# Index rows, broadcasts and network steps of a neighbour-attention kernel in another order, and the last activations on ScalarE and GpSimd

## What is computed

```python
# L0: for each point the 8 nearest points, then 4 blocks
idx = top_k(-d2(ctx), 8)
for i in range(4):
    p = where(points >= 0, points, 0.01 * points)          # the activation
    c = w_center[i] @ p                                     # here both weights are fside
    gn = w_neighbor[i] @ gather(p, idx)
    points = (c + gn.sum(over neighbours)) / 9 + points
# L1: for each point the 30 nearest points, a small network, attention
rel = pts[idx30] - pts                                      # 3 coordinates
feat = spherical(rel) and its difference from its mean      # sqrt, arctan
h = lrelu(bn(feat @ W1.T)); h = lrelu(bn(h @ W2.T)); h = lrelu(bn(h @ W3.T))
att = softmax(h); out = points + sum(att * points[idx30])
```

## Time and profile before

| what | value |
|---|---|
| median of 3 runs | 841.17 us (841.12 to 841.86) |
| the profiled execution | 846.98 us, its span 845.1 us |
| TensorE (PE) busy | 749.7 us, 89% |
| VectorE (DVE) busy | 656.1 us, 78% |
| ScalarE (ACT) busy | 260.7 us, 31% |
| GpSimd (POOL) busy | 175.3 us, 21% |
| mean granted TensorE clock | 0.949 of full speed |

### The profile page before, as it was taken

One profiled execution on the slowest core, in us unless ns is written; L12 is line 12 of the kernel. 1 busy time (PEld: TensorE's weight loads), 2 busy tenths in 40 slices (PEclk: granted clock), 3 DMA queues, 4 the chain that ended last, 5 costly groups with the idle time before them and its releaser, 6 DMA issues.

```text
span 845.1 us, 13319 instructions
## 1 busy us (share of the span) xinstructions
PE 749.7 (89%) x5530; PEld 611.5 (72%) x5530; DVE 656.1 (78%) x1057; ACT 260.7 (31%) x367; POOL 175.3 (21%) x134
## 2 busy tenths in 40 slices
PE   5979899698999999789899959794988999898988
PEld 3768788677778888678688747573876887676766
DVE  4757987969899999798897899677667878786701
ACT  7325642421551212100011221121232545454500
POOL 3113855861403113002200220121040000000000
PEclk9889899899999999999899998796999999999999
DMA  9520002020002000444430000000000455848581
GB/s 358 143 99 2 1 1 100 1 100 0 1 1 100 0 1 1 186 168 145 136 125 2 0 1 0 1 1 0 0 1 2 161 201 175 285 145 291 185 300 56
DMA packets 32700, 73.43 MB, mean 87 GB/s; under 512 B 11392, under 2 KB 11392, under 8 KB 30336
## 3 DMA queue, kind: packets, MB, share of 16 engines
q1 hardware_dynamic: 32496, 70.49, 23.9%
q10 hardware_dynamic: 144, 2.10, 0.6%
HBM read 49.37 MB, written 23.20 MB: 86 GB/s over the span
## 4 chain that ended last, share of the span: by engine, by line
PE 38%; DVE 37%; DMA 9%; ACT 7%; issue 6%; POOL 2%; SPq 0%; ACTq 0%; DVEq 0%; POOLq 0%
PE bank L1389 11%; DMA att_d<-scratch 6%; DVE scratch L937 5%; DVE idx L813 4%; DVE vals L811 4%; DVE scratch L881 3%; DVE pts_l L886 3%; PE bank L1417 3%; PE bank L1287 2%; PE bank L1368 2%; PE bank L1288 2%; PE bank L1289 2%; PE bank L1477 2%; PE bank L1369 2%; PE bank L1370 2%
## 5 line engine op out<-in xcount | busy, mean ns | idle before, releaser
L1389 PE MATMUL bank<-nbr,pts_l 128*128 128x512 f32 x1024 | 246.5, 399 | 10.5 <-DVE pts_l L886 8.2
L1389 PEld LDWEIGHTS bank<-nbr,pts_l 128*128 128x128 f32 x1024 | 194.5, 192 | 53.7 <-DVE pts_l L886 10.4
L461 POOL TENSOR_TENSOR pts_h<-scratch,pts_h 128x512 fp32r<-128x512 f32 x58 | 81.6, 1410 | 354.6 <-ACT pts_h L635 354.6
L1368 PE MATMUL bank<-wT,pts_h 128*128 128x512 f32 x256 | 105.7, 413 | 9.9 <-DVE pts_l L886 9.9
L635 ACT CAST pts_h<-scratch 128x512 fp32r<-128x512 f32 x58 | 35.9, 620 | 236.9 <-DVE scratch L881 236.9
L1369 PE MATMUL bank<-wT,pts_h 128*128 128x512 f32 x256 | 102.7, 401 | 0.0
L1370 PE MATMUL bank<-wT,pts_h 128*128 128x512 f32 x256 | 102.6, 401 | 0.0
L720 ACT COPY scratch<-bank 128x512 f32<-128x512 f32 x64 | 69.9, 1135 | 68.7 <-DMA att_d<-scratch 45.2
L1287 PE MATMUL bank<-pts_h 128*128 128x512 f32 (+2 forms) x192 | 74.5, 388 | 15.4 <-DVE pts_l L784 11.7
L642 ACT CAST pts_l<-bank 128x512 fp32r<-128x512 f32 x64 | 37.2, 588 | 135.9 <-PE bank L1370 135.7
L1288 PE MATMUL bank<-pts_l,pts_h 128*128 128x512 f32 (+2 forms) x192 | 71.0, 370 | 0.0
(11 more groups left out here) (189 smaller groups left out, 1214.4 us busy)
## 6 DMA issues: line engine op xcount, KB each, us to landing
att_d<-scratch SPq DMA_DIRECT2D x64, 256.0 KB, 2.5
nbr<-att_d SPq DMA_DIRECT2D x16, 1024.0 KB, 7.1
more<-a_rows SPq DMA_DIRECT2D x17, 480.0 KB, 4.5
scratch<-a_rows SPq DMA_DIRECT2D x15, 480.0 KB, 4.2
X<-in_ctx SPq DMA_DIRECT2D x12, 512.0 KB, 7.7
out_dram<-X SPq DMA_DIRECT2D x16, 256.0 KB, 4.6
more<-in_ctx SPq DMA_DIRECT2D x4, 512.0 KB, 7.8
scratch<-in_fside_BxSxS SPq DMA_DIRECT2D x2, 1024.0 KB, 13.5
```

The lines of the kernel that those rows point to most:

```text
L461: pool.tensor_tensor(p_l[:, t, hf * HALF:(hf + 1) * HALF], p32(n), p_h[:, t, hf * HALF:(hf + 1) * HALF].bitcast(F32), ALU.subtract).then_i ...
L1368: pe.matmul(bank[g % 3][:], p_h[:, t, cols], wT[:, 0, t, :], start=(t == 0), stop=False)
L1389: mm = pe.matmul(bank[3 + g % 3][:], y[:, m, t * P:(t + 1) * P], nbr[b][:, m, hf * HALF:(hf + 1) * HALF], start=(m == 0 and part_ == 0), s ...
```

## The change

Five things are changed.

1. The order of some calls in the set-up: `adj_turn(0)` behind `gram(2)`; on ScalarE `adjacency(1)` ahead of `mirror_out(2)`, `nbr_out(2)` behind the `high_half` copies, `adjacency(5)` and `mirror_out(9)` ahead of `gram_out(10)`, `gram_out(13)`, `mirror_out(13)` and `gram_out(14)` ahead of the first four `p_high`; on VectorE the first steps of `select` of tiles 6 and 7 behind the first four `p_make`.
2. `index_rows` at g = 36, 39, 42 and 52 with its turn one step later. SP stores the first three rows at once and starts the broadcasts then; only the broadcasts from u = 3 on wait for the whole selection. Each `lookup` waits for all four rows (`s_ar` at `CHUNKS`), `row_turned` is gone.
3. `NET` has 42 steps where it had 38: some pairs are split, an empty step stands ahead of each of the three sums, and a sum and its first reader share a step. With it `T0` goes from 109 to 113, `S0` from 115 to 119 and `S_END` from 26 to 18. The code of `FREE_AT`, `LOAD_AT` and `tail_groups` is not changed. Chunk 0 is then loaded behind q = 5, 9, 13 and 17 as before; chunk 1 behind 21, 25, 29 and 33 (before 27, 29, 31, 33), chunk 2 behind 37, 41, 45 and 49 (44, 46, 48, 50), chunk 3 behind 53, 57, 61 and 63 (59, 61, 63, 63).
4. For n >= 40 (the p of passes 5, 6 and 7) `p_make` is gone. ScalarE makes relu(x) and relu(-x/100), GpSimd subtracts them (`p_join`), and `p_high` and `p_low` follow one step later.
5. Waits that go with it (`s_sel` in `index_rows`, `s_wm` in `p_high`, `s_pr`).

```diff
+        N1 = 2 * CT * 5
+        def q32(n):
+            return more[:, 3, (n % 2) * HALF:(n % 2 + 1) * HALF]
-        R0 = 47
+        ROWS_AT = {36: 0, 39: 1, 42: 2, 52: 3}
+        TURN_AT = {g + 1: c for g, c in ROWS_AT.items()}
-        NET = [(0,), (1,), (2,), (3, 4), ((5, 0),), ((5, 1), (5, 2)), (6,), (7,), (8, (9, 0)), ((9, 1),),
-               ((9, 2), 10), (11,), (12, 13), (14, 15), (16,), (17, 18), (19,), (20, 21), (22,), (24,), (25,), (26,),
-               (27, 28), (29,), (30, 31), (32,), (33, 34), (35,), (37,), (38,), (39,), (40,), (41, 42), (44,), (45,),
-               (46,), (47,), (48,)]
+        NET = [(0,), (1,), (2,), (3, 4), ((5, 0),), ((5, 1),), ((5, 2),), (6,), (7,), (8,), ((9, 0),), ((9, 1),),
+               ((9, 2), 10), (11,), (12, 13), (14,), (15,), (16,), (17,), (18,), (19,), (20,), (21,), (22,), (),
+               (24, 25), (26,), (27, 28), (29, 30), (31, 32), (33, 34), (35,), (), (37, 38), (39,), (40,), (41, 42),
+               (), (44, 45), (46,), (47,), (48,)]
...
-            sp.wait_ge(s_adjT, TILES)
-            sp.wait_ge(s_sel, TILES)
             for c in range(CHUNKS):
-                sp.wait_ge(s_ar, c + 1)
-                sp.dma_start(a_rows[c], a_row[:]).then_inc(s_arow, 16)
-                sp.wait_ge(s_arow, 16 * (c + 1))
+                if c < CHUNKS - 1:
+                    sp.wait_ge(s_ar, c + 1)
+                    sp.dma_start(a_rows[c], a_row[:]).then_inc(s_arow, 16)
+            for c in range(CHUNKS):
                 for t in range(2 * CH):
                     u = 2 * CH * c + t
+                    if u == 0:
+                        sp.wait_ge(s_arow, 16 * (CHUNKS - 1))
                     if u == 3:
                         sp.wait_ge(s_sel, TILES)
+                    if u == 9:
+                        sp.wait_ge(s_ar, CHUNKS)
+                        sp.dma_start(a_rows[CHUNKS - 1], a_row[:]).then_inc(s_arow, 16)
+                    if u == 2 * CH * (CHUNKS - 1):
+                        sp.wait_ge(s_arow, 16 * CHUNKS)
...
+            def p_join(n):
+                pool.wait_ge(s_pr, 2 * (n - N1 + 1))
+                pool.tensor_tensor(p32(n), p32(n), q32(n), ALU.subtract).then_inc(s_p32, 1)
...
             mirror_out(1)
             gram_out(2)
             nbr_out(0)
+            adjacency(1)
             mirror_out(2)
-            adjacency(1)
...
-            nbr_out(2)
             for k in range(KT):
                 high_half(k, 1)
             mirror_out(6)
             gram_out(7)
+            nbr_out(2)
             adjacency(3)
...
             gram_out(9)
+            mirror_out(9)
             adjacency(4)
-            mirror_out(9)
+            adjacency(5)
+            gram_out(10)
+            mirror_out(10)
             nbr_out(4)
-            gram_out(10)
-            adjacency(5)
-            mirror_out(10)
...
+            def p_halves(n):
+                it = n // (2 * CT)
+                b, hf, t = it % B, (n % (2 * CT)) // CT, n % CT
+                if n == N1:
+                    act.wait_ge(s_look, 2 * TILES)
+                act.wait_ge(s_xu, 2 * CT * (it - 1))
+                act.wait_ge(s_p1, n - 1)
+                src = X[:, b, t, hf * HALF:(hf + 1) * HALF]
+                act.activation(p32(n), src, ACT.Relu).then_inc(s_pr, 1)
+                act.activation(q32(n), src, ACT.Relu, scale=-SLOPE0).then_inc(s_pr, 1)
...
             act.wait_ge(s_g, NT + 3)
+            gram_out(13)
+            mirror_out(13)
+            gram_out(14)
             for j in range(CT):
                 p_high(j)
-            gram_out(13)
+            mirror_out(14)
             adjacency(6)
-            mirror_out(13)
-            gram_out(14)
             adjacency(7)
-            mirror_out(14)
...
             select([4, 5])
-            select([6, 7], 0, 2)
...
             for n in range(CT):
                 p_make(n)
-            select([6, 7], 2, 3)
+            select([6, 7], 0, 3)
...
-                    if it + 1 < ITS:
+                    if it + 1 < ITS and 2 * CT * (it + 1) + j < N1:
                         p_make(2 * CT * (it + 1) + j)
...
             for n in range(CT):
                 w_turn(n)
+            gram(2)
             adj_turn(0)
-            gram(2)
...
-                pe.wait_ge(s_ar, row_turned(G0 + 1 + u // 2))
+                pe.wait_ge(s_ar, CHUNKS)
```

More of the change, by code:

```diff
@@ L201, in build @@
         s_p32 = sem("p_ready")
+        s_pr = sem("p_halves_ready")
         s_p0 = sem("p_high_ready")
@@ L287, in w_bank @@
             return bank[(6, 7, 4, 5, 0, 2, 6, 7)[n]][:]
-        def row_turned(g):
-            return min(max((g - R0 - 2) // 4 + 1, 0), CHUNKS)
         @block.sync
@@ L486, in _ @@
                     if s_ >= NT and it + 1 < ITS:
-                        p_low(2 * CT * (it + 1) + s_ - NT)
+                        n = 2 * CT * (it + 1) + s_ - NT
+                        if n < N1:
+                            p_low(n)
+                        else:
+                            p_join(n)
+                            if n % (2 * CT):
+                                p_low(n - 1)
+                            if n % (2 * CT) == 2 * CT - 1:
+                                p_low(n)
         @block.scalar
@@ L619, in _ @@
             gram_out(9)
+            mirror_out(9)
             adjacency(4)
-            mirror_out(9)
+            adjacency(5)
+            gram_out(10)
+            mirror_out(10)
             nbr_out(4)
-            gram_out(10)
-            adjacency(5)
-            mirror_out(10)
             gram_out(11)
             mirror_out(11)
-            norm_out(1)
             nbr_out(5)
             gram_out(12)
+            norm_out(1)
             mirror_out(12)
+            def p_halves(n):
[8 more added lines that the diff above has]
+                act.activation(q32(n), src, ACT.Relu, scale=-SLOPE0).then_inc(s_pr, 1)
             def p_high(n):
@@ L634, in p_high @@
                 act.wait_ge(s_p32, n + 1)
+                if n >= N1 and n % (2 * CT) == 0:
+                    act.wait_ge(s_wm, NT * (n // (2 * CT)))
                 act.copy(p_h[:, t, hf * HALF:(hf + 1) * HALF], p32(n)).then_inc(s_p0, 1)
@@ L665, in side @@
                     nbr_out(T)
-                if (g - R0) % 4 == 2 and 0 <= (g - R0) // 4 < CHUNKS:
-                    a_row_out((g - R0) // 4)
+                if g in TURN_AT:
+                    a_row_out(TURN_AT[g])
                 if g == 16 + NT:
@@ L751, in _ @@
                     if it + 1 < ITS:
-                        p_high(2 * CT * (it + 1) + j)
+                        n = 2 * CT * (it + 1) + j
+                        if n < N1:
+                            p_high(n)
+                        else:
+                            p_halves(n)
+                            if j:
+                                p_high(n - 1)
+                            if j == 2 * CT - 1:
+                                p_high(n)
                     side(16 * it + NT + j)
@@ L899, in index_rows @@
                 src = idx[:, CH * c:CH * (c + 1), :].rearrange("p t k -> p (t k)")
+                dve.wait_ge(s_sel, CH * (c + 1))
                 if c:
@@ L1158, in side @@
                     select_step(T, n)
-                if (g - R0) % 4 == 0 and 0 <= (g - R0) // 4 < CHUNKS:
-                    index_rows((g - R0) // 4)
+                if g in ROWS_AT:
+                    index_rows(ROWS_AT[g])
                 for u in (2 * (g - G0), 2 * (g - G0) + 1):
@@ L1399, in turn_a @@
                     pe.wait_ge(s_nbr, TILES)
-                u = min(2 * (R0 + 4 * c - G0), 2 * TILES - 2)
-                if u >= 0:
-                    pe.wait_ge(s_pick, u + 1)
                 pe.transpose(bank[6][:, 384:HALF], a_f, ident[:]).then_inc(s_aT, 1)
@@ L1433, in side @@
                     adj_turn(T)
-                if (g - R0) % 4 == 2 and 0 <= (g - R0) // 4 < CHUNKS:
-                    turn_a((g - R0) // 4)
+                if g in TURN_AT:
+                    turn_a(TURN_AT[g])
                 for u in (2 * (g - G0) - 2, 2 * (g - G0) - 1):
```

## The result

The changed kernel takes 838.68 us in the median (836.36 to 841.82, 20 runs), the kernel before, run on the same chip, 841.64 (837.48 to 846.3, 20 runs). The ratio is 0.996, with a 95% interval of 0.9944 to 0.9977: faster by some 3 us, where 10 were forecast. 838.68 lies inside the range, but nearer to no change than to the forecast. The profiled execution took 837.86 us, its span is 835.8.

A forecast was written before the change was run, and what follows sets the result against it. It saw six stretches with different limits: TensorE and VectorE full in selection, neither in lookups, TensorE partly waiting for VectorE in the network, TensorE limiting the last steps. -7 -11 -28 +36 = -10 gave 831 us, range 816 to 847.

The forecast's parts named there:

- the signs in the profile that it named: First `y_low` near 168, g 112 earlier, GpSimd some 35 us busier, four tail load waits of 6 to 8 us.
- set-up: Set-up to first `y_low`: reordered calls shorten TensorE's gaps, -3.5 -6.6 +3.5, about -7 us (bounds -3 to -10).
- rows and broadcasts: Lookups: earlier rows and broadcasts remove waits for the first broadcasts and `a_row_out`, about -11 us (-7 to -12).
- network and activation: Network and last 16 steps: 42 steps cut TensorE's idle time, -28 us, including net -2 for the moved activation.
- tail: Tail: four full TensorE stops at loads, 7.0 us each plus 2.4 of low clock; about +36 us (+23 to +45).
- The "-5" for waits that go: Tail: today's last wait (2.5 us) and some store waits vanish, since loads come every fourth spread; -5 us.
- The conversion to the runs' median: Whole kernel: the runs' median was taken as 5.8 us below the profiled 846.98, so 841.2 - 10 = 831.
- The rival of GpSimd's lock: Aggregate steps, passes 4 to 6: GpSimd's lock makes VectorE the bound; +6, 847 us; chance 0.18.
- part 3: Network and last 16 steps: `NET` with 42 steps shrinks TensorE's waits for VectorE; -28 us (bounds -5 to -45).
- Loads hidden anyway: Tail: ScalarE and SP run ahead of TensorE, so the four loads cost only 4; 799 us; chance 0.05.
- Gains cancel: Whole kernel: the passes' gain and the tail's loss cancel within 1.7 us; 841 us; chance 0.08.

The follow-up runs named there:

- the cut kernels: The kernel before and the changed kernel, each with everything behind the last `x_update` left out and X written to the output: 726.96 and 683.44 us.

## Why the prediction was wrong

Direction and mechanism were right, and the signs in the profile that it named came, but for the last stop (8.90 us, where 6 to 8 were named). It was wrong in sizes: the gain of the set-up was put too high and the cost of the tail too low, which erred the same way. Each term as forecast, by the profiled executions, and by the runs:

| term | forecast | profiles | runs |
|---|---|---|---|
| set-up | -7 | -4.6 | -2.1 and -4 to -5 |
| rows and broadcasts | -11 | -10.6 | -11.8 |
| network and activation | -28 | -29.1 | |
| these three | -46 | -44.3 | -43.5 |
| tail | +36 | +37.6 | +40.7 |
| sum | -10 | -6.7 | -2 to -3 |

The runs' -43.5 and +40.7 come from the kernels without the tail. The column of profiles takes the mean of the executions: first `y_low` at 173.1 us over six full kernels with the old set-up (171.9 to 175.5), 168.5 over nine with the new one (167.1 to 170.4); lookups' stage 248 to 251 (mean 249.8) against 237.5 to 239.5 (239.1); the stage to the last `x_update` 287.1 against 258.0; tail 133.9 against 171.5.

**The set-up** is the first step that failed. The forecast let 3.5 of the 6.12 us for `w_low` go; 1.8 went. And it read 175.5 as this kernel's set-up, while other executions had 171.9: "first `y_low` near 168" was right and the gain still too large. It also let the whole gain pass through the selection; of the 4.6 us at the first `y_low` 3.7 or 2.5 are left at the end of the fourth pass. This is 2 to 5 us.

**The tail** is the second. The four stops took 30.6 us where 4 x 7.0 = 28 were counted: the last took 8.90. The lower clock was costed rightly (0.43 against 0.24 us between products for some 6 us behind each stop). The "-5" for waits that go came about as counted: the last wait of 2.5 us is gone, and TensorE's waits for the copies fell from 6.2 to 3.5. By profiles the term is 2 short; the runs add 3 more, for which there is the indication from the cut kernels and no cause. What was seen of it: of the eight profiles of full kernels without four stops (two of them of before) the profiled execution was longer than all runs beside it in seven, by 0.8 to 9 us over their median; of the seven with four stops (three of the changed kernel) in one only. So the tail of 133.8 us that the forecast built on may itself be one that profiling lengthens; that is not shown.

**The rows' part** held to 1 us, and the first broadcast's wait went as forecast.

**The network** gave -29.1 for -28, but made up otherwise than forecast. The eight spreads alone shorten the stage by 11.6 us, where 3.8 were counted; the activation gives 3.4 (2 counted); 14 remain for the order of the pieces, where some 22 were counted. The sum came right by luck: the errors cancel.

**The conversion to the runs' median.** Taking 5.8 off was correct for before and wrong for the changed kernel, whose profiled executions lie at their median (837.86, 839.12 and 839.29 against 838.68, 839.7 and 839.92). A difference of 10 us must not be taken from one execution each where executions spread by 10 us and the profiled one can lie to one side.

**The rival of GpSimd's lock** did not happen: part 3 gave 29, far from the 18 at which it decides. The delay was 18.1 us over the 24 subtractions, where half of them at the 0.99 of the earlier trace rows, 12, was taken; that is 0.75 for each of 1.41. The Trainium skill, page SBUF — State Buffer, section Who interferes with whom, has the port locked for the whole instruction. The trace agrees where an instruction is held up: the one at 570.11 above ends with the subtraction. The 0.99 of 1.48 us in the earlier trace rows don't speak against it, since the subtraction began while the first of the two instructions ran. The forecast's 36 us (34 at 1.41) would need every subtraction to meet such an instruction from its start, and eight of 24 met none.

**Loads hidden anyway** did not happen either, and the experiments show how near it was: two steps less in `NET`, and with them `S_END` = 22, leave 3.7 us of the waits. "Gains cancel", 841, at 0.08, came nearer in time (2.3 us off) than the forecast of 831 (7.7 off), though the two don't cancel within its 1.7 us.

## What to carry to other kernels

A list of work that one loop shares with its tail has two ends: a change of the loop's length must be checked against every index that is computed from it. Here each transfer's place was computed and its consumer's was not, so a kernel could gain 44 us and give 41 back; with two steps fewer it keeps some 25. And price the terms against several executions, because a set-up or a tail of one execution can be off by more than the term.

## What the hardware showed beyond expectation

- A GpSimd subtraction of 128x512 in float32 (1.41 us) delayed VectorE by 0.75 us on average over 24 of them, more than the `p_make` it replaced cost (0.68): as a sum for VectorE the move is a loss of 1.8 us, in time a gain of about 4. The delay depends on what VectorE runs: a 128x3 instruction of 0.16 us took 1.16, until the subtraction's end, while an `x_update` beside another stayed at 0.69.
- Relu between Sqrt, Arctan and Exp needed no table of its own: the traces of both kernels have five table loads of 1.28 us.
- After a stop of 7 to 9 us TensorE's products ran at 1.2 GHz for some 6 us each time; over the tail the granted clock was 0.90 with four stops and 0.99 with none.
- Executions of one kernel on one chip spread by 10 us (838.2 to 848.6), most of the shorter ones at the higher granted clock; and without four stops in the tail the profiled execution was the longest in seven cases of eight.
